# Attention score steps that begin with the transposed products, with the mask and the scores between them and the maximum's products last

## The reference, cut to what matters

```python
x = x + jnp.tanh(g_xattn[0]) * _L0_xattn_ref(_layernorm(x, axis=-1), ctx_1024, ctx_1024, ...)
x = x + jnp.tanh(g_ffn[0]) * _L0_ffn_ref(_layernorm(x, axis=-1), ...)
x = x + jnp.tanh(g_xattn[1]) * _L1_xattn_ref(_layernorm(x, axis=-1), ctx_1024, ctx_1024, fside_BxS2_0, ...)
x = x + jnp.tanh(g_ffn[1]) * _L1_ffn_ref(x, ...)
...
scores = jnp.einsum('bhqd,bhkd->bhqk', q, k) / np.sqrt(HEAD_DIM)
scores = scores + attention_bias[:, None, None, :]
probs = jax.nn.softmax(scores, axis=-1)
out = jnp.einsum('bhqk,bhkd->bhqd', probs, v)
```

## Time and profile before

| what | value |
|---|---|
| time, median of 3 runs | 1387.45 us (1387.42 to 1388.22) |
| span of the profiled execution | 1391.8 us |
| span over the median | 4.35 us |
| TensorE matmuls busy | 95% of the span |
| VectorE, ScalarE, GpSimd busy | 67%, 57%, 51% |
| attention(0) | about 12 to 345 us of the span |
| attention(1) | about 818 to 1190 us of the span |

### The profile page before, as it was taken

How to read it: one execution, slowest core, us unless ns; L and a number is a source line. 1 busy time by engine, 2 the same in 40 slices (tenths; PEclk the granted TensorE clock), 3 DMA queues, 4 the chain that set the end, 5 groups by cost and what they waited for, 6 DMA issues and landing times.

```text
span 1391.8 us, 38216 instructions
## 1 busy us (share of the span) xinstructions
PE 1322.8 (95%) x14806; PEld 1168.8 (84%) x14806; DVE 937.1 (67%) x2484; ACT 797.0 (57%) x1759; POOL 710.3 (51%) x712
## 2 busy tenths in 40 slices
PE   7999999998899999999999978999999999899898
PEld 5888888887899999999999967888888898655476
DVE  4889898884476655555555047988888887412287
ACT  4666666662477777777776435555555555323354
POOL 2456656553277777777775044555555553200131
PEclk9999999996799999999999969999999999999999
DMA  6664545452567777777776612611111110499912
GB/s 195 226 231 166 174 147 179 157 177 65 178 211 223 222 221 224 226 227 228 227 224 242 252 42 69 241 62 47 48 48 47 47 41 17 156 404 431 370 58 69
DMA packets 103618, 237.24 MB, mean 170 GB/s; under 512 B 8976, under 2 KB 85904, under 8 KB 91024
## 3 DMA queue, kind: packets, MB, share of 16 engines
q1 hardware_dynamic: 97296, 218.02, 45.6%
q0 software_dynamic: 6144, 16.79, 3.8%
HBM read 173.96 MB, written 60.82 MB: 169 GB/s over the span
## 4 chain that ended last, share of the span: by engine, by line
PE 82%; DVE 8%; DMA 4%; issue 3%; ACT 2%; POOL 1%; SPq 0%; DVEq 0%; ACTq 0%; PEldq 0%; POOLq 0%
PE ps L1508 12%; PE psT L1493 6%; PE psS L567 5%; PE psT L576 5%; PE ps L590 5%; PE ps L782 5%; PE ps L730 4%; PE psS L1493 3%; PE ps L1493 3%; PE ps L603 3%; PE ps L744 2%; PE ps L715 2%; PE ps L654 2%; PE psT L582 2%; DMA arena<-w_dram 2%
## 5 line engine op out<-in xcount | busy, mean ns | idle before, releaser
L1461 POOL TENSOR_TENSOR wb_lo<-arena,wb_hi 128x2048 fp32r<-128x2048 f32 x64 | 296.7, 4636 | 101.1 <-ACT wb_hi L1581 101.1
L576 PE MATMUL psT<-arena 32*128 32x128 f32 x2048 | 158.9, 290 | 2.1 <-issue 0.5
L1508 PE MATMUL ps<-wb_hi,hT_hi 128*128 128x256 f32 x528 | 151.6, 287 | 2.1 <-DVE hT_lo L1634 2.1
L567 PE MATMUL psS<-arena 32*128 32x256 f32 x1024 | 151.2, 405 | 0.8 <-ACT arena L940 0.7
L1508 PE MATMUL ps<-wb_lo,hT_hi 128*128 128x256 f32 x528 | 148.5, 281 | 0.0
L1508 PE MATMUL ps<-wb_hi,hT_lo 128*128 128x256 f32 x528 | 147.7, 280 | 0.0
L576 PEld LDWEIGHTS psT<-arena 32*128 32x128 f32 x2048 | 133.2, 191 | 13.2 <-issue 12.1
L1146 POOL TENSOR_TENSOR arena<-arena,eps_sb 128x1 f32<-128x1 f32 x96 | 26.3, 273 | 225.5 <-DVE arena L1020 139.1
L1581 ACT CAST wb_hi<-arena 128x1024 fp32r<-128x1024 f32 x128 | 130.7, 1045 | 11.0 <-DMA arena<-w_dram 10.5
L567 PEld LDWEIGHTS psS<-arena 32*128 32x128 f32 x1024 | 92.9, 191 | 14.5 <-issue 11.6
L1646 DVE TENSOR_TENSOR arena<-ps,arena 128x512 f32<-128x512 f32 (+1 forms) x39 | 25.4, 650 | 114.9 <-PE ps L1508 74.5
(11 more groups left out here) (375 smaller groups left out, 3954.2 us busy)
## 6 DMA issues: line engine op xcount, KB each, us to landing
arena<-wset_dram SPq DMA_DIRECT2D x24, 2048.0 KB, 14.8
xs_rows<-arena SPq DMA_DIRECT2D x33, 1024.0 KB, 8.2
arena<-w_dram SPq DMA_DIRECT2D x32, 1028.0 KB, 6.0
arena<-w_dram SPq DMA_DIRECT2D x32, 1024.0 KB, 5.9
arena<-w_dram SPq DMA_DIRECT2D x7, 2052.0 KB, 12.2
w_sb<-xs_rows SPq DMA_DIRECT2D x33, 256.0 KB, 2.7
xs_rows<-arena SPq DMA_DIRECT2D x33, 256.0 KB, 5.5
arena<-ctxT_dram SPq DMA_DIRECT2D x63, 128.0 KB, 2.4
```

The source lines that it names most:

```text
L567: last = nc.tensor.matmul(psS[:, b, c * D:(c + 1) * D], qT[p, k % 3, c, :], kbd[p, k % 3, c, :, :], start=A, stop=A or c == 1, skip_group_ ...
L576: nc.tensor.matmul(psT[:, b, j * P:(j + 1) * P], kbd[p, (k - 1) % 3, c, par, :], qT[p, (k - 1) % 3, c, :], start=j == 0, stop=False, skip_ ...
L1461: nc.gpsimd.tensor_tensor(wb_lo[:, u % 2, part], wb_raw[:, u % 2, part], wb_hi[:, u % 2, part], ALU.subtract).then_inc(w_g.sem, 1)
L1508: last = nc.tensor.matmul(ps[5][:, t * D:(t + 1) * D], hp[:, f, t * P:(t + 1) * P], wp[:, f, :], start=f == 0 and t == 0 and n == 0, stop= ...
```

## The change

The score step is written in another order. It begins with the transposed products j = 0, for which it waits only for `ex_a`. Then come the waits for `pre_a`, `kv_a` and `mx_v` and the mask, the transposed products j = 1, the upright products c = 0, the transposed products j = 2 and 3, the upright products c = 1, and, behind the wait for `m_a` in h = 0, the products of `pick` and `mT`. Number, kind and shape of the matmuls are the same, and so is every other engine's program.

```diff
+                    if valid(k - 1):
+                        if h == 0:
+                            before(pe, ex_a.sem, ex_a.at(k - 2, "b"))
+                        else:
+                            pe.wait_ge(ex_a.sem, ex_a.at(k - 1, "a"))
+                        transposed(0)
                     if valid(k):
                         if h == 0:
                             pe.wait_ge(pre_a.sem, pre_a.at(k, "Q"))
...
                     if valid(k - 1):
+                        transposed(1)
+                    if valid(k):
+                        upright(0)
+                    if valid(k - 1):
+                        transposed(2)
+                        transposed(3)
+                    if valid(k):
+                        upright(1)
+                    if valid(k - 1):
                         if h == 0:
                             pe.wait_ge(m_a.sem, m_a.at(k - 1, "mT"))
-                            before(pe, ex_a.sem, ex_a.at(k - 2, "b"))
-                        else:
-                            pe.wait_ge(ex_a.sem, ex_a.at(k - 1, "a"))
-                    for c in range(C):
-                        if valid(k):
-                            for b in range(2):
...
-                            if c == 1:
-                                last.then_inc(s_p.sem, 1)
-                        if valid(k - 1):
-                            for par in range(2):
```

More of the change, by code:

```diff
@@ L541, in scores @@
                 def scores(k, h):
+                    def transposed(j):
+                        c, par = j // 2, j % 2
+                        for b in range(2):
+                            p = slice(32 * (2 - 2 * h + b), 32 * (2 - 2 * h + b) + 32)
+                            nc.tensor.matmul(psT[:, b, j * P:(j + 1) * P], kbd[p, (k - 1) % 3, c, par, :],
+                                             qT[p, (k - 1) % 3, c, :], start=j == 0, stop=False, skip_group_check=True)
+                    def upright(c):
+                        for b in range(2):
+                            p = slice(32 * (2 * h + b), 32 * (2 * h + b) + 32)
+                            last = nc.tensor.matmul(psS[:, b, c * D:(c + 1) * D], qT[p, k % 3, c, :],
+                                                    kbd[p, k % 3, c, :, :], start=A, stop=A or c == 1, skip_group_check=True)
+                        if c == 1:
+                            last.then_inc(s_p.sem, 1)
+                    if valid(k - 1):
[4 more added lines that the diff above has]
+                        transposed(0)
                     if valid(k):
@@ L557, in scores @@
                     if valid(k - 1):
+                        transposed(1)
[7 more added lines that the diff above has]
+                    if valid(k - 1):
                         if h == 0:
                             pe.wait_ge(m_a.sem, m_a.at(k - 1, "mT"))
-                            before(pe, ex_a.sem, ex_a.at(k - 2, "b"))
-                        else:
-                            pe.wait_ge(ex_a.sem, ex_a.at(k - 1, "a"))
-                    for c in range(C):
-                        if valid(k):
-                            for b in range(2):
-                                p = slice(32 * (2 * h + b), 32 * (2 * h + b) + 32)
-                                last = nc.tensor.matmul(psS[:, b, c * D:(c + 1) * D], qT[p, k % 3, c, :],
-                                                        kbd[p, k % 3, c, :, :], start=A, stop=A or c == 1, skip_group_check=True)
-                            if c == 1:
-                                last.then_inc(s_p.sem, 1)
-                        if valid(k - 1):
-                            for par in range(2):
[L573 to L578, removed]
                         for j in range(4):
```

## The result

The changed kernel is slower. Its four timed runs are 1393.89 to 1404.19 us, median 1399.05, beside 1387.43 for the kernel before; the ratio is 1.0086, 95% interval 1.0044 to 1.0129 (+12 us, 6 to 18). The profiled execution is the one of 1404.19 us.

What follows compares the result with a forecast made beforehand. TensorE's program was taken to set the time, VectorE close behind. Earlier transposed products (-1.2 us) and later upright ones (+0.6 us) summed to -0.6 us: 1387.45 to 1386.9, rounded to 1387 us; range 1383 to 1397.

Steps and rivals of the forecast that it cites:

- reason against the pauses: TensorE's 26 pauses of 0.94 us in attention(1) might come from recording: at least 4.35 us of the span were untimed.
- rivals with real pauses: Attention(1) pauses exist in timed runs: slower through GpSimd's loop, 1390 to 1399 us (0.28), or a gain, 1381.5 us (0.15).
- term for the upright products in attention(0): Upright products start 0.02 us later, delaying VectorE's chain to L700: 30 x 0.02 = +0.6 us; bounds 0 and +3 us.
- loop over GpSimd: Rival, attention(1): gather, TensorE, VectorE loop sets the 11.59 us step; +0.44 us a step, +11.4 us, 1399 us; chance 0.28.
- first term: Attention(1), distance from a gather's end to VectorE's first maximum L1000: 1.30 us, growing towards 1.7 us if pauses are real.
- Strict order: Rival: last upright products cannot start before last transposed ones; 0.24 us later, +7 us in attention(0), 1394.5 us; chance 0.07.
- score step without a pause: Sign in the changed profile: where there is no pause, h = 0 and h = 1 take 1.31 to 1.33 us.
- term of -1.2 us: Attention(1): transposed products start 0.02 us earlier in h = 0 and h = 1 of some 31 steps each; bounds 0, -2.5 us.
- Waiting later for `m_a`: Wait moved from the first upright product to the last eight: 0 us; if it did bind, the new place could only be better.

Runs made afterwards that it cites:

- U1 one place earlier: Changed kernel with the upright products c = 1 moved between the transposed products j = 2 and 3; 1.0067 of the kernel before, +9.3 us.
- the earlier gathers: Kernel before with attention(1)'s gathers issued three GpSimd operations sooner, ahead of the context split and bias addition; ratio 0.9828, -23.9 us.
- the run of both together: Kernel before with gathers three GpSimd operations sooner and the order j = 0, mask, c = 0, j = 1, c = 1, j = 2 and 3; 0.9828, 1364.5 us.
- the order with early upright products: Changed kernel reordered to j = 0, mask, c = 0, j = 1, c = 1, j = 2 and 3, late `m_a` wait kept; 0.9974 of the kernel before.

## Why the prediction was wrong

The forecast was no change, 1387 us; the time is 1399, 2 us above the range.

**The reason against the pauses failed.** "At least 4.35 us of the span were not in them" took one execution's length for the cost of recording. Time and span differ by 1.85 to 2.17 us in every run that gives both, and taking the pauses away won 23.9 us in the timed runs. On this step I gave the rivals with real pauses less than half, and sized the forecast as if score steps were undisturbed.

**The term for the upright products in attention(0) was mis-sized.** Its mechanism, VectorE's chain to L700, was right; the term was 30 x 0.02 = 0.6 us, taken from the upper pairs of the earlier trace rows. The last pair starts 0.13 us late, the late undisturbed steps lose 0.12 us each, and all steps of attention(0) outside 8 to 23 lose 1.4 us. That is near the bound that I had given and not taken, 0.1 us a step if the last pair has to wait until one more transposed quartet has half gone by. With U1 one place earlier the late steps are back at 9.55 us.

**A whole group of steps was missing.** In steps 8 to 23 a scatter ends at the score step, and the sum has no term for it. In the old order it cost nothing, so no wait of the maximum showed it: the upright products went on almost at their pace, and VectorE was not held. In the new order TensorE pauses ahead of all of them. I had looked for pauses only where they cost, in the earlier trace rows, and let speak for all of attention(0). These 16 steps lose 0.35 us each, 5.6 us, the largest part of the loss.

**The loop over GpSimd was real and its price wrong.** That it sets the step while there are gathers is shown by the earlier gathers, which brought the step from 11.58 to 10.67 us. In the changed kernel its first term grew from 1.30 to a mean of 1.41 us in the two steps shown, not by 0.44. I had held TensorE's place against the gather fixed. In fact a later pause leaves TensorE further ahead in the next step (0.74 and 1.14 us ahead of the gather's end against 0.47), and then more products get through. 26 x 0.1 us is 2 to 3 us, not 11.4. So the time that this rival gave, 1399, came true by luck: the loss lies in attention(0), for which the rival had no term.

**Strict order** came half true. The last upright pair starts with the last transposed one and not behind it, 0.13 us late and not 0.24; and the first one starts 0.03 us into the step, ahead of the pair T1 that stands before it in the program. The Trainium skill, "TensorE: Matmul & The Clock Gate", Part 3 (The mechanism), has matmuls start strictly in program order. The trace after does not agree for the first pair, and is close to it for the last. How far a row group may run ahead I did not measure, beyond the run with all upright products first: there the transposed rows start with six upright rows that stand ahead of them still to come.

**What held.** The score step without a pause takes 1.31 us, and the transposed products' earlier start is worth 0.04 to 0.05 us a step of attention(1): it shows in the time of a step once the pauses are gone, 10.67 to 10.62 us and, in the run of both together, (1089.9 - 877.6) / 20 = 10.62 again. That is what the term of -1.2 us said, by one execution of the old order and two that begin with T0. With pauses it bought nothing that the runs show. Waiting later for `m_a` lost nothing as part of the order with early upright products; by itself it was not tried.

## What to carry to other kernels

A stall that costs nothing today belongs in the account of a reordering as much as one that costs: look at each stretch for what gets through ahead of it, and put there what another engine waits for. Where a loop over several engines closes to a hundredth, price a change in it only after asking what the other engine does with the time it is given, and attack its longest term first: issuing each step's gathers three GpSimd operations sooner was worth 23.9 us, twice what the new order of the score step lost. Compare a profiled span with the run's own time before calling any part of it recording.

## What the runs showed of the hardware

Where the row of GpSimd's second indirect transfer of a step ends 0.09 to 1.14 us into the score step, TensorE stops and goes on 0.40 to 0.44 us behind the end of that row, with gathers (1001.14 to 1001.54) and scatters (209.09 to 209.50) alike. Where it ends just as the score step starts (204.39 and 204.40), TensorE hardly stops: its next rows come at 204.72 and 204.85. How many matmul rows get through first depends on how far ahead it was: 6 rows with the score step 0.47 us ahead of the gather's end, 10 with 0.74 us. The end of a transfer alone does not stop it. With the earlier gathers the second row ends at 1004.96, just ahead of the output products (1004.98), and these take 1.08 us and the score step 1.33, as where nothing is in the way. What the pause is made of, the rows don't tell: no semaphore is charged with it, and no run here separates the matmuls from their reports.
